# Moving the moment matmuls within a slot of the output phase

## The chip, the cores and the metric

The kernel runs on one core of a Trainium2 chip. The time is the device time of one execution in microseconds (us). TensorE is called PE in the rows, VectorE DVE, ScalarE ACT, GpSimd POOL, and SyncE SP. SP does no arithmetic here: it issues the DMAs.

## What is computed

The reference is a chain of blocks on a tensor of 16 images of 64 x 64 tokens with 128 channels. The change touches the last step of the attention block and the batch statistics that the block after it needs:

```python
attn1 = jax.nn.softmax(sim1, axis=-1)          # sim1 = q @ k_landmarks, 8 heads of 16, 64 landmarks
out = attn1 @ attn2_inv @ (attn3 @ v)          # attn2_inv @ (attn3 @ v) is ready before the output phase
res = conv_general_dilated(v, conv_w, ...)     # along the tokens, 33 taps per head
out = (out + res).reshape(...) @ w_out + b_out
t = t + out
...
Wx = jnp.einsum('bti,hi->bth', _ln_t(t), W)    # the ffn
mean = jnp.mean(flat, axis=0)                  # over all tokens of all images
var = jnp.var(flat, axis=0)
```

The mean and variance of `Wx` follow from the first and second moments of the normalised tokens. The kernel gathers these moments while it makes the tokens.

## The kernel before

The program runs its phases one after the other: group norm, the recurrent layer, landmarks, the pseudo-inverse, the output phase, and a last recurrence over the tokens. The edit lies in `output_phase` (from L1878).

The output phase goes over 16 images, each in 8 groups of 512 tokens. The work on one group is spread over several **slots**, and a slot (b, c) does one step each of several groups: 128 slots in all. On each engine a function `slot` writes out the order by hand, and semaphores tie the engines together. There is no scheduler. The names below are the tiles in the rows.

TensorE's slot, in its order before the change, with the line of each matmul:

- `scores` (L2171, L2175): the attention scores of group c, four banks of 512 columns (`o_bank_s`). They wait for ScalarE's negated maxima, and for its copies out of the banks that they overwrite: the third is the bank of the convolution (semaphore `convc`, set by ScalarE's copy at L2289).
- `row_maxima` r = 0 (L2152): half of the scores of group c + 1 in bf16, from which VectorE takes row maxima (L2355). Its banks are two, `o_bank_l`.
- `project` (L2211): the output projection of group c - 3 into `o_bank_x`.
- `row_maxima` r = 1 (L2152): the other half, into the same two banks. The second bank may be written only when VectorE has read two maxima of r = 0.
- `weigh` (L2185): the weighing of the values with the exponentials, which waits for ScalarE's four exponentials (L2318) and overwrites two of the score banks.
- `queries` (L2138) of group c + 3, `turn_maxima` (L2160) of group c + 1, `convolve` (L2197) for the next image, and `turn_convolved` (L2205), transposes of the convolved values of group c - 2.
- `moments` (L2224): 16 small matmuls of group c - 4 that add into `o_bank_m`, which is read once, at the phase's end. They wait for GpSimd's scaled tokens `o_u` (L2089), written in the slot's first microseconds.

ScalarE's slot: four exponentials (L2318), two scalings of the residual's base (L2302), the rounded queries (L2295), the two copies of the weighed values `o_even` and `o_odd` (L2310, L2312), the queries (L2280), the negated maxima (L2284), the convolved values (L2289), two more scalings.

VectorE's slot: the four maxima of group c + 1 (L2355), the residual of group c - 3 with its statistics (L2366 to L2372), the reciprocals of the packed denominators (L2386, which wait for a DMA), normalising (L2397), adding the convolved values (L2380, which waits for the transposes of `turn_convolved`), and merging (L2391). Of these, normalising and merging read two operands from SBUF.

GpSimd's slot: the mask (L2073), then variance plus epsilon (L2082), the power (L2084) and the scaled tokens (L2089) of group c - 3, then the base's bias (L2097).

SyncE's queue: the reciprocals are spread and broadcast through DRAM, and the next denominators are packed after that, so that one reciprocals instruction stands a whole chain of DMAs behind the one before it.

The last image has no `convolve`, and the first four slots have no `moments`.

Of the kernel before, what the change touches and what calls it, by code (L numbers as in the profile page):

```python
# [1877 lines left out]
def output_phase(nc, sems, R, E, K, xnt, tokens, vals, recips, scaled):  # L1878


    with ExitStack() as ctx:
# [47 lines left out]
        def nth(b, c):  # L1929

            return NG * b + c + 1

        def wait(eng, name, count):

            if count > 0:
                eng.wait_ge(s[name], count)
# [13 lines left out]
        def follows(c, k, last):  # L1950

            return c + k < NG or not last

        def precedes(c, k, first):

            return c >= k or not first
# [171 lines left out]
        def _(pe):  # L2128
# [5 lines left out]
            def queries(b, c):  # L2134

                pe.wait_ge(*loaded(s_xl, *at(b, c)))
                wait(pe, "qc", nth(b, c) - 1)
                nc.tensor.matmul(bank_q[:, :], w[:, :], xnT[c % 4][:, :], start=True, stop=True).then_inc(s["qm"], 1)  # L2138

            def row_maxima(b, c, r, q):  # L2140

                if r == 0:
                    wait(pe, "ql", nth(b, c))
                    wait(pe, "setup", SETUP * (b + (c == NG) + 1))
                    wait(pe, "neg", nth(b, c) - 1)
                for k in range(2):
                    for half in range(2):
                        if k == 0:
                            wait(pe, "max", GT * (nth(b, c) - 1) + 2 * r + half - 1)
                        rows, heads = slice(LM * half, LM * half + LM), slice(PAIRS_H * half, PAIRS_H * half + PAIRS_H)  # L2150
                        token = P * (2 * r + k)
                        ml = nc.tensor.matmul(bank_l[half][:, 2 * P * k:2 * P * k + 2 * P], q_lp[c % 2][rows, token:token + P],  # L2152
                                              kb_lp[q][rows, heads, :].rearrange("c h l -> c (h l)"), start=True, stop=True)
                        if k == 1:
                            ml.then_inc(s["lp"], 1)

            def turn_maxima(b, c):
                wait(pe, "max", GT * nth(b, c))
                for k in range(GT):
                    mt = nc.tensor.matmul(bank_l[0][:, P * k:P * k + P], m1[:, k, :], E.ident_lp[:, :], start=True, stop=True)  # L2160
                mt.then_inc(s["mt"], 1)

            def scores(b, c, q):

                wait(pe, "neg", nth(b, c))
                wait(pe, "denc", 2 * (nth(b, c) - 1))
                wait(pe, "qc", min(nth(b, c) + 2, B * NG))
                wait(pe, "convc", min(NG + nth(b, c) - 1, B * NG))
                for g in range(PAIRS_H):
                    rows = slice(QUAD * g, QUAD * g + QUAD)  # L2170
                    nc.tensor.matmul(bank_s[g][:, :], ind[rows, :, :].rearrange("c a l -> c (a l)"), negm[c % 2][rows, :],  # L2171
                                     start=True, stop=False)
                for g in range(PAIRS_H):
                    rows = slice(QUAD * g, QUAD * g + QUAD)
                    ms = nc.tensor.matmul(bank_s[g][:, :], kb[q][rows, :, :].rearrange("c a l -> c (a l)"), qT[c % 4][rows, :],  # L2175
                                          start=False, stop=True)
                ms.then_inc(s["s1"], 1)

            def weigh(b, c, q):

                wait(pe, "exp", PAIRS_H * nth(b, c))
                for h in range(2):
                    rows = slice(LM * h, LM * h + LM)
                    for g in range(PAIRS_H):
                        mp = nc.tensor.matmul(bank_pv[h][QUAD * g:QUAD * g + QUAD, :], zb[q][rows, g, :], p1[g][rows, :],  # L2185
                                              start=True, stop=True)
                mp.then_inc(s["pv"], 1)

            def convolve(b, c, out):

                half, pair = c // GT, c % GT
                pe.wait_ge(s_v[half], 128 * (b + 1))
                turns = out.rearrange("p (n e) -> p n e", e=2 * DH)
                for a in range(2):
                    h = 2 * pair + a
                    for side in range(2):
                        mm = nc.tensor.matmul(turns[LM * side:LM * side + LM, :, DH * a:DH * a + DH], bands[:, h, :],  # L2197
                                              v[half][side][:, :, (DH + 1) * h:(DH + 1) * h + DH], start=True, stop=True,
                                              skip_group_check=True)
                mm.then_inc(s["conv"], 1)  # L2200

            def turn_convolved(b, c, q):
                wait(pe, "res", nth(b, c) - 1)
                for k in range(GT):
                    mt = nc.tensor.transpose(bank_x[:, k, :], res[q][:, GT * (c % NG) + k, :], R.ident[:, :])  # L2205
                mt.then_inc(s["ct"], 1)

            def project(b, c):
                wait(pe, "add", nth(b, c))
                for k in range(GT):  # L2210
                    mt = nc.tensor.matmul(bank_x[:, k, :], oT[:, P * k:P * k + P], wo[:, :], start=True, stop=True)  # L2211
                mt.then_inc(s["wo"], 1)

            def moments(b, c):

                n = nth(b, c)
                wait(pe, "u", n)
                if n == 1:
                    pe.wait_ge(K.ready, K.PARTS + 2)
                    wait(pe, "centre", 2)  # L2220
                for k in range(GT):
                    for g in range(P // QUAD):
                        r = (g - k) % BLOCK_ROWS
                        mm = nc.tensor.matmul(bank_m[QUAD * g:QUAD * g + QUAD, FROM[r]:FROM[r] + WIDTH[r]],  # L2224
                                              u[c % 2][:, k, 1 + QUAD * r:1 + QUAD * r + QUAD], u[c % 2][:, k, 0:WIDTH[r]],
                                              start=n == 1 and k == 0, stop=n == B * NG and k == GT - 1, skip_group_check=True)
                mm.then_inc(s["moments"], 1)

            def slot(b, c, q, first, last):
                scores(b, c, q)  # L2230
                nq = q if c + 1 < NG else 1 - q
                if follows(c, 1, last):
                    row_maxima(b, c + 1, 0, nq)
                if precedes(c, 3, first):
                    project(b, c - 3)
                if follows(c, 1, last):
                    row_maxima(b, c + 1, 1, nq)
                weigh(b, c, q)
                if follows(c, 3, last):
                    queries(b, c + 3)  # L2240
                if follows(c, 1, last):
                    turn_maxima(b, c + 1)
                if not last:
                    convolve(b + 1, c, bank_conv[:, :])
                if precedes(c, 2, first):
                    turn_convolved(b, c - 2, q if c >= 2 else 1 - q)
                if precedes(c, 4, first):
                    moments(b, c - 4)

            nc.tensor.matmul(bank_m[:, 0:C], E.avg[:, :], fw[:, :], start=True, stop=True).then_inc(s["centre"], 1)  # L2250
            pe.wait_ge(s_band, 16)
# [8 lines left out]
            turn_maxima(0, 0)  # L2260
            wait(pe, "convc", NG)
            each_image(pe, slot)
            project(B - 1, NG - 3)
            turn_convolved(B - 1, NG - 2, 1)
# [594 lines left out]
```

## Time and profile before

| | us |
|---|---|
| median of 3 runs | 5903.51 |
| lowest, highest | 5903.4, 5907.3 |
| the profiled execution | 5913.64 |
| its span (first to last instruction) | 5911.8 |
| output phase, first to last slot's work, by the stage rows | about 1078 |

The stages of the trace are told apart by the lines that run. The output phase takes the stretch from 2515 to 3593 us of the span; what stands before and after it uses none of the changed lines. A slot is read from one engine at a time: the timeline of TensorE gives each slot from one `scores` (L2171) to the next, and the timelines of the other engines over the same stretch show what each was doing meanwhile.

### The profile page before, as it was taken

Reading aid. Unit: us, or ns where it says so; the run is one execution under the profiler, and the core shown is the slowest. Engines: PE = TensorE matmul, PEld = TensorE weight load, DVE = VectorE, ACT = ScalarE, POOL = GpSimd, SP = SyncE. Lnnn points to the kernel's source line nnn. Section 1 sums busy time; section 2 is a strip of 40 time slices with the busy share of each in tenths; the row PEclk is TensorE's granted clock in tenths of the full one; section 3 lists DMA queues with packets and bytes.
Section 4 is the critical chain, followed back from the end, with each engine's and each line's share of the span. In section 5 each row is a group of like instructions: output and inputs, shape, how many; then the busy total and the mean of one; then the engine's idle time right before and its main releaser. Section 6 shows DMA issues by size and latency. Waiting matters only on the chain. (4 is left out here: it accounts for less than half of the span.)

```text
span 5911.8 us, 223297 instructions
## 1 busy us (share of the span) xinstructions
PE 5253.6 (89%) x97395; PEld 3278.2 (55%) x97488; DVE 3071.2 (52%) x8152; ACT 3138.0 (53%) x9108; POOL 1523.0 (26%) x1905
## 2 busy tenths in 40 slices
PE   5599999997899998799999997888888888888888
PEld 4599888896566666744444444333333333333333
DVE  8677777775788886568888883111111111111111
ACT  6465555565677776378888883333333333333333
POOL 2100000002888874256666662000000000000000
PEclk7899999999999999999999998999999999999999
DMA  9631111225777773467777762111111111111100
GB/s 389 270 115 58 58 58 60 84 77 183 245 245 243 231 243 105 102 175 203 202 203 202 204 173 66 33 34 32 32 34 33 32 32 35 32 32 32 35 18 24
DMA packets 773031, 689.32 MB, mean 117 GB/s; under 512 B 67056, under 2 KB 663024, under 8 KB 767984
## 3 DMA queue, kind: packets, MB, share of 16 engines
q1 hardware_dynamic: 754672, 575.39, 32.6%
q0 software_dynamic: 14672, 95.16, 4.0%
q8 instruction: 743, 12.17, 0.9%
q10 hardware_dynamic: 2736, 4.89, 0.2%
q14 instruction: 208, 1.70, 0.1%
HBM read 392.17 MB, written 274.89 MB: 113 GB/s over the span
## 5 line engine op out<-in xcount | busy, mean ns | idle before, releaser
L2797 ACT ACTIVATE f_y<-f_acc 128x16 f32<-128x16 f32 x4096 | 754.7, 184 | 1542.5 <-PE f_acc L2739 1542.5
L2739 PEld LDWEIGHTS f_acc<-f_y,f_vT 128*32 128x32 f32 x32768 | 645.2, 108 | 1438.7 <-ACT f_y L2797 1437.0
L2739 PE MATMUL f_acc<-f_y,f_vT 128*32 128x16 f32 x32768 | 1046.1, 193 | 279.6 <-issue 1.5
L2697 PE MATMUL f_junk<-f_idle 128*32 128x512 bf16 x8400 | 832.5, 376 | 0.0
L2579 DVE COPY f_zT<-f_zt 128x512 f32<-128x512 f32 x124 | 85.8, 692 | 1138.4 <-PE f_zt L2653 1138.4
L2355 DVE TENSOR_REDUCE o_m<-o_bank_l 128x8 bf16<-128x512 f32 x512 | 329.7, 686 | 132.4 <-PE o_bank_l L2152 130.0
L2572 DVE TENSOR_SCALAR f_wxn<-f_wxp,f_scale,f_shift 128x512 f32<-128x512 f32 x126 | 102.1, 811 | 509.0 <-PE f_wxp L2667 508.9
L1299 ACT ACTIVATE a_p<-a_s 128x512 f32<-128x512 f32 x502 | 259.3, 602 | 153.0 <-PE a_s L1166 151.2
L2318 ACT ACTIVATE o_p<-o_bank_s 128x512 f32<-128x512 f32 x512 | 264.4, 602 | 142.0 <-PE o_bank_s L2175 142.0
L533 POOL DMA_DIRECT2D hidden<-l_h x46 | 34.7, 756 | 1162.1 <-DVE l_hsum L790 961.6
L712 ACT ACTIVATE l_gate<-l_pf,r_ctx 128x256 f32<-128x256 f32 (+7 forms) x512 | 202.5, 446 | 229.1 <-PE l_pf L643 228.8
L2592 DVE SCALAR_TENSOR_TENSOR f_sum<-f_u,f_std,f_turned 128x128 f32<-128x128 f32 x512 | 143.6, 344 | 317.9 <-PE f_turned L2690 317.9
L2697 PEld LDWEIGHTS f_junk<-f_idle 128*32 128x32 bf16 x8400 | 250.0, 99 | 0.0
L1359 DVE TENSOR_REDUCE a_m3p<-a_s 128x1 f32<-128x512 f32 x360 | 223.6, 684 | 50.8 <-PE a_s L1126 49.4
L633 PE MATMUL l_pio<-l_x,r_k_lm 128*128 128x256 f32 (+7 forms) x1024 | 239.0, 356 | 0.2 <-ACT l_gate L729 0.2
L633 PE MATMUL l_pf<-l_x,r_k_lm 128*128 128x256 f32 (+7 forms) x1024 | 238.9, 356 | 0.0
L647 PE MATMUL l_pio<-l_hsum,r_ctx 128*128 128x256 f32 (+7 forms) x1024 | 238.8, 356 | 0.0
L2302 ACT ACTIVATE o_base<-o_base,r_loss,r_gain 128x128 f32<-128x128 f32 x512 | 225.8, 498 | 0.3 <-DMA o_base<-tokens 0.3
L2690 PE MATMUL f_turned<-f_ident,f_y 128*32 128x128 f32 x4096 | 221.1, 290 | 0.5 <-DVE f_sum L2592 0.5
L1017 POOL TENSOR_TENSOR a_r<-a_vare,a_half 128x8 f32<-128x8 f32 x128 | 209.6, 1638 | 10.0
L712 ACT ACTIVATE l_gate<-l_pio,r_ctx 128x256 f32<-128x256 f32 (+7 forms) x512 | 203.4, 450 | 13.9
L2679 PE MATMUL f_acc<-f_wxn,f_ident 128*32 128x128 f32 x4096 | 207.1, 274 | 0.7 <-issue 0.7
(323 smaller groups left out, 11517.6 us busy)
## 6 DMA issues: line engine op xcount, KB each, us to landing
o_v<-vals SPq DMA_DIRECT2D x256, 272.0 KB, 3.4
a_hid<-hidden SPq DMA_DIRECT2D x112, 520.0 KB, 5.0
hidden<-l_h POOLq DMA_DIRECT2D x46, 1040.0 KB, 6.6
l_x<-skew SPq DMA_DIRECT2D x46, 1024.0 KB, 5.2
vals<-a_v SPq DMA_DIRECT2D x128, 272.0 KB, 3.4
gn_x<-in_x SPq DMA_DIRECT2D x16, 2048.0 KB, 17.4
a_xin<-in_x SPq DMA_DIRECT2D x128, 256.0 KB, 5.1
tokens<-a_t SPq DMA_DIRECT2D x128, 256.0 KB, 3.4
```

What stands on the lines that cost most here:

```text
L633: mm = nc.tensor.matmul(banks[c][g][:, :, rows], w[W[g]], xs, start=g in (0, 2, 3), stop=False, skip_group_check=True)
L647: mm = nc.tensor.matmul(banks[c][g][:, :, rows], w[U[g]], hsum[:, lanes[c], rows], start=False, stop=True, skip_group_check=True)
L712: nc.scalar.activation(gate[:, g, lanes[c], rows], banks[c][g][:, :, rows], ACT.Tanh if g == 2 else ACT.Sigmoid, bias=bias[BI[g]]).then_in ...
L1299: nc.scalar.activation(p3[c % 2][g][:, :], score_bank(i, c, g), ACT.Exp).then_inc(s["exp"], 1)
L1359: nc.vector.tensor_reduce(m3p[:, g, c:c + 1], bank[:, :], AX.X, ALU.max).then_inc(s["mx"], 1)
L2302: nc.scalar.activation(bs[c % 4][:, k, :], bs[c % 4][:, k, :], ACT.Identity, scale=R.gain[:, b, n:n + 1], bias=R.loss[:, b, n:n + 1]).then ...
L2318: nc.scalar.activation(p1[g][:, :], bank_s[g][:, :], ACT.Exp).then_inc(s["exp"], 1)
L2355: nc.vector.tensor_reduce(m1[:, 2 * r:2 * r + 2, LM * half:LM * half + LM].rearrange("p k (g r) -> p k g r", r=QUAD)[:, :, :, 0:2], bank_l ...
L2690: mt = nc.tensor.matmul(turned[g % 2][rows, b % 4, :], y[q][:, rows, b], ident[:, :], start=True, stop=True)
L2697: nc.tensor.matmul(junk[rows, :], idle[:, 0:QUAD], idle[:, :], start=True, stop=True)
L2739: mm = nc.tensor.matmul(acc[k % 2][rows, t, :], vT[:, rows], before, start=False, stop=True, skip_group_check=True)
L2797: nc.scalar.activation(y[q][:, step, :], acc[step // RC % 2][:, step % RC, :], ACT.Sigmoid).then_inc(s_y, 1)
```

## The change

In TensorE's slot, the call of `moments(b, c - 4)` moves from the last place to the place between `row_maxima` r = 1 and `weigh`. No instruction is added or removed, and the order on ScalarE, VectorE, GpSimd and SyncE is the same.

```diff
@@ -2235,6 +2235,8 @@
                     project(b, c - 3)
                 if follows(c, 1, last):
                     row_maxima(b, c + 1, 1, nq)
+                if precedes(c, 4, first):
+                    moments(b, c - 4)
                 weigh(b, c, q)
                 if follows(c, 3, last):
                     queries(b, c + 3)
@@ -2244,8 +2246,6 @@
                     convolve(b + 1, c, bank_conv[:, :])
                 if precedes(c, 2, first):
                     turn_convolved(b, c - 2, q if c >= 2 else 1 - q)
-                if precedes(c, 4, first):
-                    moments(b, c - 4)
```

TensorE before, the first slot that has moments, from its scores to the first moment matmuls:

```order
L2171 MATMUL o_bank_s<-o_negm,o_ind 128x512 x4
L2175 MATMUL o_bank_s<-o_qT,o_kb 128x512 x4
L2152 MATMUL o_bank_l<-o_kb_lp,o_q_lp 128x256 x4
L2211 MATMUL o_bank_x<-o_wo,o_oT 128x128 x4
L2152 MATMUL o_bank_l<-o_kb_lp,o_q_lp 128x256 x4
L2185 MATMUL o_bank_s<-o_p,o_zb 32x512 x8
L2138 MATMUL o_bank_s<-o_xnT,o_wq 128x512
L2160 MATMUL o_bank_l<-o_ident_lp,o_m 128x128 x4
L2197 MATMUL o_bank_s<-o_v,o_bands 64x16x16 x4
L2205 MATMUL o_bank_x<-r_ident,o_res 128x128 x4
L2224 MATMUL o_bank_m<-o_u 32x33
L2224 MATMUL o_bank_m<-o_u 32x65
```

TensorE now, the same slot, from its scores to the first moment matmuls:

```order
L2171 MATMUL o_bank_s<-o_negm,o_ind 128x512 x4
L2175 MATMUL o_bank_s<-o_qT,o_kb 128x512 x4
L2152 MATMUL o_bank_l<-o_kb_lp,o_q_lp 128x256 x4
L2211 MATMUL o_bank_x<-o_wo,o_oT 128x128 x4
L2152 MATMUL o_bank_l<-o_kb_lp,o_q_lp 128x256 x4
L2224 MATMUL o_bank_m<-o_u 32x33
L2224 MATMUL o_bank_m<-o_u 32x65
```

The moments stand where the weighing stood, and the weighing comes behind them. TensorE now, from the last moment matmul to the next slot's scores:

```order
L2224 MATMUL o_bank_m<-o_u 32x33
L2185 MATMUL o_bank_s<-o_p,o_zb 32x512 x8
L2138 MATMUL o_bank_s<-o_xnT,o_wq 128x512
L2160 MATMUL o_bank_l<-o_ident_lp,o_m 128x128 x4
L2197 MATMUL o_bank_s<-o_v,o_bands 64x16x16 x4
L2205 MATMUL o_bank_x<-r_ident,o_res 128x128 x4
L2171 MATMUL o_bank_s<-o_negm,o_ind 128x512 x4
```

The next scores (L2171) now follow the transposes (L2205) directly.

## Rows read from the trace of the kernel before

**Rows 1.** Stages of the output phase: stretch, us, busy us by engine, PEclk, DMA, GB/s.

```profile
2561.30:3510.30 949.00, 917.92 (x10908) 469.42 (x10911) 782.82 (x1973) 784.15 (x1626) 636.00 (x640) 1.00 0.72 200
3510.30:3593.50 83.20, 65.48 (x835) 38.22 (x830) 61.86 (x167) 47.05 (x100) 54.12 (x54) 0.86 0.38 107
```

**Rows 2.** Timeline, PE, one steady slot: start us, us, what, [idle before].

```profile
2856.58 0.40 PE L2171 MATMUL o_bank_s<-o_negm,o_ind 32*128 32x512 bf16 x4
...
2859.18 0.75 PE L2152 MATMUL o_bank_l<-o_kb_lp,o_q_lp 64*128 64x256 bf16 x4
2860.03 1.09 PE L2185 MATMUL o_bank_s<-o_p,o_zb 64*32 64x512 f32 x16
...
2863.37 0.66 PE L2205 MATMUL o_bank_x<-r_ident,o_res 128*128 128x128 f32 x4
2863.95 0.77 PE L2224 MATMUL o_bank_m<-o_u 128*32 128x33 f32 x32
2864.66 0.40 PE L2171 MATMUL o_bank_s<-o_negm,o_ind 32*128 32x512 bf16 x4
```

**Rows 3.** Timeline, ACT, the same slot: the exponentials.

```profile
2857.91 2.06 ACT L2318 ACTIVATE o_p<-o_bank_s 128x512 f32<-128x512 f32 x4 [1.14 <-PE o_bank_s L2175]
```

**Rows 4.** Timeline, PE, the last slot that has no moments.

```profile
2553.66 0.40 PE L2171 MATMUL o_bank_s<-o_negm,o_ind 32*128 32x512 bf16 x4 [0.20 <-ACT o_res L2289]
...
2557.09 1.09 PE L2185 MATMUL o_bank_s<-o_p,o_zb 64*32 64x512 f32 x16
...
2561.32 0.40 PE L2171 MATMUL o_bank_s<-o_negm,o_ind 32*128 32x512 bf16 x4 [0.20 <-ACT o_res L2289]
```

**Rows 5.** Timeline, ACT, that slot's copy of the convolved values.

```profile
2560.57 0.60 ACT L2289 ACTIVATE o_res<-o_bank_s 128x512 f32<-128x512 f32 x1 [0.21 <-PE o_bank_s L2197]
```

**Rows 6.** Timeline, DVE, the end of that slot: adding and merging.

```profile
2561.21 0.69 DVE L2380 TENSOR_TENSOR o_oT<-o_att,o_bank_x 128x512 f32<-128x512 f32 x1 [0.23 <-DVE o_att L2397]
2561.81 0.74 DVE L2391 SCALAR_TENSOR_TENSOR o_att<-o_odd,o_keep,o_pvs 128x512 f32<-128x512 f32 x1
```

**Rows 7.** Timeline, DVE, the steady slot of rows 2.

```profile
2856.65 0.74 DVE L2391 SCALAR_TENSOR_TENSOR o_att<-o_odd,o_keep,o_pvs 128x512 f32<-128x512 f32 x1
2858.19 1.29 DVE L2355 TENSOR_REDUCE o_m<-o_bank_l 128x8 bf16<-128x512 f32 x2 [0.80 <-PE o_bank_l L2152]
...
2861.07 0.68 DVE L2366 TENSOR_TENSOR o_t<-o_bank_x,o_base 128x512 f32<-128x512 f32 x1
```

**Rows 8.** Timeline, POOL, the scaled tokens at this slot's start and the next one's.

```profile
2857.02 1.27 POOL L2089 TENSOR_TENSOR o_u<-o_t,k_rstd 128x512 f32<-128x512 f32 x1
...
2865.12 1.25 POOL L2089 TENSOR_TENSOR o_u<-o_t,k_rstd 128x512 f32<-128x512 f32 x1
```

**Rows 9.** Timeline, DVE, a slot in which the merging took long.

```profile
3052.53 1.61 DVE L2391 SCALAR_TENSOR_TENSOR o_att<-o_odd,o_keep,o_pvs 128x512 f32<-128x512 f32 x1
3054.07 1.28 DVE L2355 TENSOR_REDUCE o_m<-o_bank_l 128x8 bf16<-128x512 f32 x2
```

**Rows 10.** Timeline, POOL, the scaled tokens of that slot.

```profile
3052.56 1.04 POOL L2089 TENSOR_TENSOR o_u<-o_t,k_rstd 128x512 f32<-128x512 f32 x1
```

**Rows 11.** Timeline, PE, that slot: scores, then the rest of the second row maxima.

```profile
3052.12 0.40 PE L2171 MATMUL o_bank_s<-o_negm,o_ind 32*128 32x512 bf16 x4
...
3055.40 0.39 PE L2152 MATMUL o_bank_l<-o_kb_lp,o_q_lp 64*128 64x256 bf16 x3 [0.32 <-DVE o_m L2355]
```

**Rows 12.** Timeline, DVE, a slot with late reciprocals.

```profile
2590.05 0.68 DVE L2366 TENSOR_TENSOR o_t<-o_bank_x,o_base 128x512 f32<-128x512 f32 x1
...
2592.49 0.35 DVE L2386 RECIPROCAL o_rec_packed<-o_den_packed 128x32 f32<-128x32 f32 x1 [0.40 <-DMA o_den_packed<-o_odd]
...
2594.02 1.12 DVE L2391 SCALAR_TENSOR_TENSOR o_att<-o_odd,o_keep,o_pvs 128x512 f32<-128x512 f32 x1
```

**Rows 13.** Timeline, POOL, the scaled tokens of that slot.

```profile
2593.55 1.04 POOL L2089 TENSOR_TENSOR o_u<-o_t,k_rstd 128x512 f32<-128x512 f32 x1
```

**Rows 14.** Waits from 2561 to 3510 us: total, times, longest.

```profile
DVE o_rec_packed L2386 <- DMA o_den_packed<-o_odd: 29.1, 41, 2.2
```

**Rows 15.** Timeline, PE: scores at both ends of one of the long slots.

```profile
2626.02 0.40 PE L2171 MATMUL o_bank_s<-o_negm,o_ind 32*128 32x512 bf16 x4
...
2635.40 0.39 PE L2171 MATMUL o_bank_s<-o_negm,o_ind 32*128 32x512 bf16 x4
```

**Rows 16.** Timeline, PE, the scores of the last image's first slot.

```profile
3510.28 0.40 PE L2171 MATMUL o_bank_s<-o_negm,o_ind 32*128 32x512 bf16 x4
```

## The prediction, made before the changed kernel ran

> **What bounds the kernel now.** I read the stages first, then one slot engine by engine. The changed lines run in the output phase alone. There TensorE is busy for 917.9 of 949.0 us with the clock granted in full, and VectorE and ScalarE for 783 and 784 [rows 1], so TensorE's order sets the pace and the other two have about a sixth of the time to spare. Next comes TensorE's timeline of a steady slot. From one scores (L2171) to the next it takes 2864.66 - 2856.58 = 8.08 us [rows 2]; in the neighbouring slots 8.08 and 8.10 take turns, and I calculate with 8.09. I cut the slot at the weighing (L2185). The first part, scores to weighing, takes 3.45 us [rows 2]. It ends with the exponentials, which begin 1.33 after the scores and are done at 3.39 [rows 3]. The second part, weighing to the next scores, takes 4.63 us, and its last piece is the moments, 2864.66 - 2863.95 = 0.71 us [rows 2]. TensorE waits nowhere in the second part.
>
> The first four slots have no moments, and their rows show what binds once they are gone from the slot's end. The second part took 2561.32 - 2557.09 = 4.23 us there [rows 4], and ended with a wait of 0.20 for ScalarE's copy of the convolved values, which ran until 2561.17 [rows 5]. The scores overwrite that copy's bank. This copy stands behind four other ScalarE instructions that begin when the weighing ends, so it moves with the weighing. The slots beside it show 4.19; I use 4.21.
>
> **The change part by part.** Nothing is added or removed. The moments' 0.71 us leave the second part and enter the first one.
>
> *Second part.* 0.71 us go, but only 4.64 - 4.21 = 0.43 is won, since the wait for the convolved copy appears in their place. The copy had been hidden by the moments alone.
>
> *First part.* The second row maxima end at 2859.93, 3.35 after the scores, and the exponentials end at 3.39 [rows 2, 3]. The idle time into which the moments could go is thus 0.1 us (2859.93 to 2860.03). There is also a pause of 0.36 inside the second row maxima (four of these matmuls take 0.75 here and 0.39 unhindered, as the three and the lone one of rows 11 show), where TensorE waits for VectorE's second maximum. The moments stand behind that pause, not in it. So the weighing starts 3.35 - 0.07 + 0.71 = 3.99 after the scores, where 0.07 is the overlap by which each group follows the last (the transposes end at 2864.03, and the moments start at 2863.95). The exponentials then end 0.6 us before they are wanted, which gives nothing back. The first part grows by 0.54.
>
> A slot would then take 3.99 + 4.21 = 8.20 us, 0.11 more than now, if VectorE kept up as before. It doesn't, by these rows.
>
> *VectorE against GpSimd.* The merging (L2391) starts 0.60 after the adding (L2380), and the adding follows the transposes, which come a fixed time after the weighing. In the slot without moments it started 4.72 us after the weighing (2561.81 against 2557.09) and so 0.49 after the next scores [rows 4, 6]. With moments it starts just 0.07 after the scores (2856.65 against 2856.58), since the scores themselves are later [rows 2, 7]. The scaled tokens (L2089) on GpSimd hang from something else: they start 4.05 us after the residual (2865.12 against 2861.07), and that starts 1.14 after the second row maxima end [rows 2, 7, 8]. Now the merging has a lead of 0.37 (2856.65 against 2857.02), takes 0.74, and GpSimd's instruction is the one that is stretched, to 1.27 from 1.04 [rows 7, 8, 10].
>
> After the change the merging starts at 0.49 of a slot, and the scaled tokens at 1.14 + 4.05 - 0.64 - 4.21 = 0.34, where 0.64 is what lies between the end of the row maxima and the weighing. GpSimd is first, by 0.15. What this costs stands in two places. With a lead of 0.03 only, the merging took 1.61 and ended 0.54 after GpSimd's instruction (3054.14 against 3053.60) [rows 9, 10]. With GpSimd 0.47 ahead it took 1.12 and ended 0.55 behind it (2595.14 against 2594.59) [rows 12, 13]. So the merging ends at 0.34 + 1.04 + 0.55 = 1.93 of the slot. The first maximum follows 0.07 before that end, as at 3054.07 [rows 9]: at 1.86, where now it starts at 1.61 (2858.19) [rows 7]. The second row maxima then end 1.72 later (3055.79 against 3054.07) [rows 9, 11], at 3.58 in place of 3.35. The slot takes 3.58 - 0.07 + 0.71 + 4.21 = 8.43 to 8.44 us. The delay moves residual, scaled tokens, weighing and merging alike, so the 0.15 stays and the collision returns in the next slot.
>
> For VectorE's wait the Trainium skill has a rule (page "SBUF — State Buffer", section "Who interferes with whom"): a VectorE instruction with two SBUF inputs and a GpSimd instruction that reads SBUF exclude each other, and the second to issue waits until the first is finished. This agrees with which instructions were stretched. It would have the merging start anew at GpSimd's end, with its whole 0.74 behind it, 0.19 later than the 0.55 of rows 9 and 10; by it a slot would take 8.63 and the sum would come to some +48 us. The rows decide here.
>
> *Not all slots collide.* Where the reciprocals wait for their DMA (41 waits of 29.1 us in all [rows 14]), normalising comes later and the power on GpSimd gets through before it: the scaled tokens then start 3.50 after the residual (2593.55 against 2590.05 [rows 12, 13]) instead of 4.05. In the changed kernel they would end at -0.21 + 1.04 = 0.83 of the slot, and the merging at 0.83 + 0.55 = 1.38, early enough for the maxima at 1.61. Such a slot takes 8.20. Of the 116 slots with moments outside the last image, 42 were of this kind. The chain of DMAs from one reciprocals instruction to the next is as long as before while the slots are longer, so there are fewer of them. I carried the distances between reciprocals of the trace through the changed slot times; some 85 slots came out at 8.44, some 30 at 8.20 to 8.4 (8.25 in the mean), and one long one.
>
> *Long slots.* Some slots take much more than 8.09 where the broadcast reciprocals come late (9.38 from 2626.02 to 2635.40 [rows 15]). All excess over 8.09 together is 10.5 us. The adding waits for the transposes, and now these come 0.54 later as seen from the residual, so lateness up to that is absorbed. I keep one of 9.4.
>
> *Moved past nothing else.* The moments wait for scaled tokens that are done about 1.4 us into the slot and are wanted at 3.3, so this wait costs nothing, with 1.9 us of cover; what queues behind it is the weighing. Their bank is read at the phase's end. SP's queue is not touched.
>
> *Last image.* It has no convolution, so the negated maxima bind in the second part instead. Its seven slots grow by up to 0.5 each, but in the trace they are stretched by late reciprocals anyway (83 us for the tail with the last slots [rows 1]). I take +1, between 0 and +3.
>
> *Sum.* Before: 3510.28 - 2561.32 = 948.96 us for 116 slots [rows 4, 16], 8.18 each. After: 85 x 8.44 + 30 x 8.25 + 9.4 = 974.3. Difference +25.3, with the last image +26. On the profiled execution, span 5911.8 and time 5913.64, that gives 5937.8 and 5939.6; on the median of 5903.51 it gives 5929.5, say **5930 us** (+0.45%). That execution lies 10 us above the median, and I have no row that puts this difference in the output phase.
>
> **The rivals.**
>
> *No collision: no change.* The 0.15 us between GpSimd and the merging is a difference of two sums of eight terms. If the moments take 0.19 less in their new place, or the convolved copy 0.19 less, the merging gets ahead and a slot takes 8.20. For it: in the trace of before the merging is ahead in two slots of three. Against: a lead of 0.03 wasn't enough [rows 9, 10], and no single term is uncertain by 0.1. Price: 116 x 8.20 = 951.2, with two long slots 954, +1: +3 to +6 us, 5908.
>
> *Faster.* The moments could fill the time in which TensorE waits before the weighing, 0.1 for the exponentials and 0.36 for the maximum, which is what a total of waits suggests. They would then cost the first part nothing, and the second wins its 0.43: 116 x 7.66 = 889, 5903.5 - 60 = 5844. The pause would have to lie behind the moments. It lies ahead of them and the idle time there is 0.1 [rows 2, 3]. This decides from a first part under 3.88.
>
> *Slower than forecast.* Every slot collides: 116 x 8.44 = 979.0, +31, 5935. If the merging is held back for its whole length, as in the rule above, 5952.
>
> **How the numbers follow.** A measurement of this kernel can tell about 0.2%, 11.8 us, from no change. Chances: collision in most slots 0.75, no collision 0.18, faster 0.04, the whole-length case 0.03. The collision case alone spans 5917 to 5942 (half of the slots at 8.20, or all at 8.44 with 0.05 more each). The range takes in the no-collision case down to 5906 and goes to 5945. Faster than -0.2%: 0.04. Within: 0.18. Slower: 0.78.
>
> **What the changed profile would show.** In a steady slot: weighing 3.99 to 4.2 after the scores; scores that follow the transposes with an idle time of about 0.2 released by the convolved copy; no wait of the weighing for the exponentials; the merging at about 1.4 us instead of 0.75, starting 0.15 behind the scaled tokens; the wait for VectorE's maximum in the second row maxima longer by a quarter microsecond; slots of 8.44 in most places and 8.20 where the reciprocals waited; fewer waits of the reciprocals than 41. The forecast is wrong if the merging stays at 0.75 with GpSimd's instruction stretched (no change), or if the weighing keeps 3.45.

## The result and the profile after

| | before | after |
|---|---|---|
| median, us | 5907.30 (5 runs) | 5939.63 (5 runs) |
| lowest, highest | 5903.40, 5914.07 | 5935.92, 5943.66 |
| ratio, 95% interval | | 1.0054 [1.0039, 1.0068] |
| span of the profiled execution | 5911.8 | 5939.1 |
| the 116 slots of [rows 4, 16] | 948.96 | 973.63 |

The kernel became slower by 32 us. 5930 was forecast, with a range of 5906 to 5945. In the profiled executions the spans differ by 27.3 us, and 24.7 of these lie in the 116 slots with moments outside the last image. The rest isn't the edit's: in the profiles of this study the first slot began anywhere between 2527 and 2538 us, whatever the output phase held. I therefore compare variants by those 116 slots, and give the median beside them. Each of these sums is from one profiled execution, so I read nothing into a difference of a few microseconds between two of them; each ratio of an experiment is to the kernel before on the same chip.

The stage row of after answers to [rows 1]: stretch, us, busy us of PE, PEld, DVE, ACT and POOL, PEclk, DMA, GB/s.

```profile
2566.40:3540.00 973.60, 917.61 (x10904) 474.27 (x10905) 826.46 (x1973) 785.37 (x1625) 667.04 (x640) 1.00 0.70 196
```

TensorE and ScalarE are as busy as before (917.9, 784.2), at the full clock. VectorE counts 44 us more and GpSimd 31 more, with the same number of instructions. So some of theirs take longer: the merging adds up to 158.6 us where it was 98.9, and GpSimd's bias of the base (L2097), which stands right behind the scaled tokens, to 196.9 where it was 166.5. The scaled tokens themselves take less, 122.6 us where it was 138.7. The timeline of TensorE shows a slot, as [rows 2] did (start us, us, what, [idle before]).

```profile
2868.39 0.40 PE L2171 MATMUL o_bank_s<-o_negm,o_ind 32*128 32x512 bf16 x4 [0.20 <-ACT o_res L2289]
...
2870.99 0.28 PE L2152 MATMUL o_bank_l<-o_kb_lp,o_q_lp 64*128 64x256 bf16 x1
2871.57 0.39 PE L2152 MATMUL o_bank_l<-o_kb_lp,o_q_lp 64*128 64x256 bf16 x3 [0.30 <-DVE o_m L2355]
2871.89 0.77 PE L2224 MATMUL o_bank_m<-o_u 128*32 128x33 f32 x32
2872.59 1.09 PE L2185 MATMUL o_bank_s<-o_p,o_zb 64*32 64x512 f32 x16
...
2875.93 0.66 PE L2205 MATMUL o_bank_x<-r_ident,o_res 128*128 128x128 f32 x4
2876.78 0.40 PE L2171 MATMUL o_bank_s<-o_negm,o_ind 32*128 32x512 bf16 x4 [0.20 <-ACT o_res L2289]
```

The moments take 2872.59 - 2871.89 = 0.70 us in the new place, as in the old one. The weighing comes 4.20 after the scores, where it came at 3.45. It was 2876.78 - 2872.59 = 4.19 from there to the next scores, where it was 4.63, and the scores now wait 0.20 for ScalarE's copy of the convolved values. The second row maxima stand still for VectorE in the middle and end at 2871.96, 3.57 after the scores and not 3.35.

VectorE's timeline over the same slot says why (it answers to [rows 6, 7]):

```profile
2868.28 0.69 DVE L2380 TENSOR_TENSOR o_oT<-o_att,o_bank_x 128x512 f32<-128x512 f32 x1 [0.79 <-DVE o_att L2397]
2868.89 1.43 DVE L2391 SCALAR_TENSOR_TENSOR o_att<-o_odd,o_keep,o_pvs 128x512 f32<-128x512 f32 x1
2870.24 1.28 DVE L2355 TENSOR_REDUCE o_m<-o_bank_l 128x8 bf16<-128x512 f32 x2
```

And GpSimd's (it answers to [rows 8]):

```profile
2868.73 1.04 POOL L2089 TENSOR_TENSOR o_u<-o_t,k_rstd 128x512 f32<-128x512 f32 x1
2869.72 1.71 POOL L2097 TENSOR_TENSOR o_base<-o_base,o_bout 128x512 f32<-128x512 f32 x1
```

The scaled tokens start at 2868.73, 0.34 after the scores. The merging starts at 2868.89, 0.16 behind them, and takes 1.43 us. It ends 0.55 after the scaled tokens (2870.32 against 2869.77). The maxima start 1.85 into the slot instead of 1.61. In the next slot the merging stands 0.13 behind and the slot takes 8.45; the two kinds take turns. In the trace of before the merging led by 0.37 and took 0.74 [rows 7, 8].

The table of waits of after, over the 116 slots, holds the rest (total, times, longest):

```profile
PEld o_bank_l L2152 <- DVE o_m L2355: 54.3, 116, 0.5
PE o_bank_s L2171 <- ACT o_res L2289: 23.4, 116, 0.2
DVE o_rec_packed L2386 <- DMA o_den_packed<-o_odd: 2.8, 9, 0.6
```

The row maxima wait 0.47 us a slot for VectorE's maxima, and the scores wait for the convolved copy in all 116 slots. The reciprocals waited 9 times for 2.8 us, where it had been 41 times for 29.1 [rows 14].

### The profile page after: what moved, and what is told of

Same layout as the page of the kernel before. It is cut to its first block and busy times, and to the rows that moved or that the text cites. A ratio compares the mean times of both kernels' runs of the same rounds, so it can differ in the third digit from the quotient of the medians.

```text
span 5939.1 us, 223297 instructions
## 1 busy us (share of the span) xinstructions
PE 5252.7 (88%) x97395; PEld 3284.8 (55%) x97488; DVE 3115.5 (52%) x8152; ACT 3138.1 (53%) x9108; POOL 1552.9 (26%) x1905
## 5 line engine op out<-in xcount | busy, mean ns | idle before, releaser
L2097 POOL TENSOR_TENSOR o_base<-o_base,o_bout 128x512 f32<-128x512 f32 x128 | 213.9, 1671 | 4.0 <-ACT o_base L2302 4.0
```

## The experiments

The theory, *collision*: the move alone costs 0.11 us a slot (0.54 lost in the first part, 0.43 won in the second), and most slots lose another 0.24, since the merging on VectorE and the scaled tokens on GpSimd hold each other up and the order of their starts has turned round. The first rival, *order alone*: VectorE is late behind TensorE for a reason of its own, and GpSimd has no part in it. The second doubts a step: the moments could have been hidden in the first part after all.

### GpSimd is given more to do: nap

The changed kernel, with a memset of a tile that nobody reads:

```diff
+                pool.memset(nap[:, :], 0.0)                  # nap: [P, 256]
                 pool.tensor_tensor(u[c % 2][:, :, 1:1 + C], t2s[c % 2][:, :, :], ...
```

> The changed kernel, with one memset of an unused tile of 128 x 256 fp32 put on GpSimd right before its scaled tokens: work is added, nothing else moves. Theory (collision): in the changed kernel the scaled tokens start at 0.37 of a slot and the merging at 0.50, so the merging waits and a slot takes 8.40 to 8.45. If the memset delays the scaled tokens by more than 0.15 us, the merging comes first and takes 0.75, the second row maxima end at 3.35, and a slot takes 8.17 to 8.20. Over 116 slots that is 27 us less than the changed kernel: added work makes it faster, at about 5912, +5 us against the kernel before. If the memset takes less than 0.13, nothing changes. Rival (TensorE's order alone, the merging is late for a reason of its own): the slots stay at 8.43, 5938 or more. Rival (GpSimd is itself late for something): slower than the changed kernel.

Measured: 5918.3 us, ratio to before 1.0015 [1.0006, 1.0025]; 952.7 us for the 116 slots, 20.9 less than the changed kernel. GpSimd's timeline:

```profile
2863.98 0.31 POOL L2090 MEMSET o_nap<- 128x256 f32 x1
2864.25 1.55 POOL L2091 TENSOR_TENSOR o_u<-o_t,k_rstd 128x512 f32<-128x512 f32 x1
```

VectorE's:

```profile
2864.16 0.75 DVE L2393 SCALAR_TENSOR_TENSOR o_att<-o_odd,o_keep,o_pvs 128x512 f32<-128x512 f32 x1
2865.27 1.29 DVE L2357 TENSOR_REDUCE o_m<-o_bank_l 128x8 bf16<-128x512 f32 x2 [0.37 <-PE o_bank_l L2154]
```

The merging now leads by 0.09 and takes 0.75. GpSimd's instruction is the one that is stretched, to 1.55, which hurts nobody. 107 of the slots take 8.17 to 8.20, the other nine more. The 27 us that were expected were not quite reached. More work on GpSimd made the kernel faster, and order alone cannot explain that.

### The same with a short memset: short_nap

```diff
-        nap = m.sb("o_nap", [P, 256])
+        nap = m.sb("o_nap", [P, 64])
```

> As the run nap, with a memset of 64 columns in place of 256. The long one delayed the scaled tokens by 0.25 us. Theory (collision, decided by who starts first): this one delays them by 0.05 to 0.10, and in the changed kernel they lead the merging by 0.12 to 0.15; so they still come first, the merging still waits and ends 0.55 after them, that is later by the delay. A slot gets longer by it, 8.47 to 8.53 in place of 8.40 to 8.45, 979 to 988 over the 116 slots, 5945 to 5953. Rival (any work on GpSimd spreads the two apart gradually): between the changed kernel and nap, 8.3 to 8.4. The same edit with more columns took 21 us away, so a sign that turns round with the size of the memset would speak for the order of starts alone.

Measured (4 runs): 5946.4 us, ratio 1.0063 [1.0047, 1.0079]; 982.05 us for the 116 slots, 8.4 more than the changed kernel. GpSimd's timeline, and the merging of the same slot:

```profile
2910.67 0.15 POOL L2090 MEMSET o_nap<- 128x64 f32 x1
2910.78 1.04 POOL L2091 TENSOR_TENSOR o_u<-o_t,k_rstd 128x512 f32<-128x512 f32 x1
```

```profile
2910.82 1.54 DVE L2393 SCALAR_TENSOR_TENSOR o_att<-o_odd,o_keep,o_pvs 128x512 f32<-128x512 f32 x1
2912.28 1.27 DVE L2357 TENSOR_REDUCE o_m<-o_bank_l 128x8 bf16<-128x512 f32 x2
```

The delay is 0.08, and the scaled tokens still lead, by 0.04. The merging takes 1.54 and ends 0.54 after them. In 101 slots the mean is 8.51 us, against 8.43 in the 98 colliding slots of the changed kernel. A delay of 0.08 costs 8 us and one of 0.25 gives 21 back: the sign turns where the order of the starts turns.

### The merging is moved out of the way: merge_first, before_merge_first

```diff
                 if precedes(c, 2, first):
                     normalise(b, c - 2)
-                    add_convolved(b, c - 2)
                 if precedes(c, 1, first):
                     merge(b, c - 1)
+                if precedes(c, 2, first):
+                    add_convolved(b, c - 2)
```

On the changed kernel:

> The changed kernel, with VectorE's merging of group c - 1 put between normalising and adding, so that it no longer starts behind the transposes, some 0.5 after the scores, but right after normalising, 2.85 after the residual. Theory (collision): the merging then meets the power on GpSimd (2.95 after the residual) with a lead of 0.1, and the scaled tokens later start while VectorE has no instruction with two operands from SBUF; the maxima start at 1.61, a slot takes 8.17 to 8.20, 27 us less than the changed kernel, about 5912. Rival (TensorE's order alone): 8.43 stays.

Measured: 5913.53 us, ratio 1.0012 [1.0003, 1.0021]; 950.0 us for the 116 slots, 23.6 less than the changed kernel. VectorE's timeline:

```profile
2866.74 0.74 DVE L2391 SCALAR_TENSOR_TENSOR o_att<-o_odd,o_keep,o_pvs 128x512 f32<-128x512 f32 x1
2867.55 0.69 DVE L2380 TENSOR_TENSOR o_oT<-o_att,o_bank_x 128x512 f32<-128x512 f32 x1
2869.27 1.29 DVE L2355 TENSOR_REDUCE o_m<-o_bank_l 128x8 bf16<-128x512 f32 x2 [1.03 <-PE o_bank_l L2152]
```

The maxima start 1.61 after the scores at 2867.66, released by TensorE alone. It is 3.98 from scores to weighing and 4.20 from there on in the median: the 8.17 to 8.20 that a slot takes with the move and without the collision. That is 0.10 more than in the kernel before, and yet all 116 slots together take only 1.0 us more (950.0 against 948.96): the kernel before had 10.5 us of slots that were longer than 8.09, and these have all but gone. The same edit on the kernel before:

> The kernel before with the merging put ahead of the adding, the edit that took 24 us from the changed kernel. Theory (that edit removes the collision and nothing else): in the kernel before the merging mostly came first anyway, so at most the long slots change; 8.08 to 8.10 a slot, 938 to 949 over 116 slots, 0 to -10 us. Rival (merging early is a gain of its own): -20 us or more, 5885.

Measured: 5911.91 us, ratio 1.0002 [0.9992, 1.0011]; 946.95 us for the slots, 2.0 less. The merging placed early is no gain of its own. It only takes away a collision, and there was little of one.

### The moments ahead of the pause: in_pause

The moments one place further up than in the changed kernel:

```diff
                     project(b, c - 3)
+                if precedes(c, 4, first):
+                    moments(b, c - 4)
                 if follows(c, 1, last):
                     row_maxima(b, c + 1, 1, nq)
```

> The moments stand one place earlier than in the changed kernel: between the projection and the second row maxima, ahead of the pause in which TensorE waits for VectorE's second maximum. My step said that the moments gain nothing in the first part because the pause lies ahead of them. Theory: here they fill the pause. Projection ends at 2.67, moments until 3.31, the four row-maxima matmuls then take 0.32 unhindered, weighing at 3.63 in place of 3.98 to 4.23. The second part stays at 4.2 (the convolved copy). 7.84 by TensorE's order; the merging leads the scaled tokens by 0.5, no collision. Then the chain of DMAs between reciprocals (7.4 to 9.5, where it is seen, 8.2 in the middle) becomes the next bound: I expect 7.9 to 8.1 a slot, 5885 to 5905, faster than the kernel before by 0 to 20 us. Rival (the first part cannot take the moments anywhere): slots of 8.2 or more, 5915 and above.

Measured: 5899.09 us, ratio 0.9989 [0.998, 0.9998]; 936.9 us for the 116 slots, 12.1 less than before. TensorE's timeline:

```profile
2581.78 0.40 PE L2171 MATMUL o_bank_s<-o_negm,o_ind 32*128 32x512 bf16 x4 [0.20 <-ACT o_res L2289]
...
2584.38 0.77 PE L2224 MATMUL o_bank_m<-o_u 128*32 128x33 f32 x32
2585.08 0.39 PE L2152 MATMUL o_bank_l<-o_kb_lp,o_q_lp 64*128 64x256 bf16 x4
2585.41 1.09 PE L2185 MATMUL o_bank_s<-o_p,o_zb 64*32 64x512 f32 x16
...
2589.63 0.40 PE L2171 MATMUL o_bank_s<-o_negm,o_ind 32*128 32x512 bf16 x4 [0.20 <-ACT o_res L2289]
```

The four row-maxima matmuls run through in 0.39 where they took 0.75, the weighing comes 3.63 after the scores, and the slot takes 7.85. So the same 0.70 us of matmuls cost 0.54 in the first part behind the pause and 0.18 ahead of it. The forecast's step was right: behind the row maxima the moments gain nothing. Ahead of them there is no collision in such a slot either: the merging starts 0.59 before the scaled tokens (2582.36 against 2582.95). Of the possible 40 us, though, only 12 came. The waits hold the rest, and there are two kinds:

```profile
DVE o_rec_packed L2386 <- DMA o_den_packed<-o_odd: 43.4, 65, 2.2
PE o_bank_s L2197 <- DMA o_v<-vals: 9.3, 10, 1.6
```

99 slots take 7.89 in the mean, 4 some 8.5, and 13 take 122.3 us together, 9.4 each. In six of the 13 the first part is long (5.1 to 5.5 us) and no load is waited for: TensorE's projection waits for VectorE's adding, as in the slot of [rows 15]. In the other seven TensorE itself waits in the second part, in `convolve`, for the load of the next image's values, as here in a slot of 9.30:

```profile
2852.26 1.11 PE L2197 MATMUL o_bank_s<-o_v,o_bands 128*64 128x256 f32 x8 [0.98 <-DMA o_v<-vals]
```

The ten slots with that wait hold 12 of the 27.5 us by which the 116 slots exceed 7.84 each. In the kernel before there were three such slots, with 1.9 us of waits. Both kinds are waits for DMAs that the longer slots seldom met. That the chain from one reciprocals instruction to the next takes longer than such a slot fits the first kind (7.3 to 9.4 us where the reciprocals waited); what makes the loads late, no run shows.

### Half and half, and nearly none: halves, few_moments

```diff
                     project(b, c - 3)
+                if precedes(c, 4, first):
+                    moments(b, c - 4, range(2))
...
                 if precedes(c, 4, first):
-                    moments(b, c - 4)
+                    moments(b, c - 4, range(2, GT))
```

> Two of the four token tiles' moments (8 of 16 matmuls, 0.35 us) stand between the projection and the second row maxima, the other two stay at the slot's end. Theory: the first half fills the pause of 0.36 for the second maximum, so the weighing stays at 3.45. The second half covers the wait for the convolved copy: weighing to scores 3.93 + 0.35 = 4.28 in place of 4.64. A slot takes 7.73 by TensorE's order, if nothing else binds; I expect the DMA chain between the reciprocals to bind then, at 7.9 to 8.1, 5885 to 5905. The second part at 4.28 would show that the copy needs 0.3 of cover and that 0.35 of it is as good as 0.71. Rival (moments cost their 0.71 wherever they stand): 8.09, 5905.

Measured: 5901.65 us, ratio 0.9991 [0.9982, 1.0], which reaches no change; 942.0 us for the 116 slots. Most slots take 7.9, and ten take over 9, with both kinds of waits again. The weighing stayed at 3.45 as expected. The second part was 4.46, not 4.28, since half of the moments takes more than half of the time:

```profile
2697.78 0.59 PE L2224 MATMUL o_bank_m<-o_u 128*32 128x33 f32 x16
2698.31 0.39 PE L2152 MATMUL o_bank_l<-o_kb_lp,o_q_lp 64*128 64x256 bf16 x4
2698.63 1.09 PE L2185 MATMUL o_bank_s<-o_p,o_zb 64*32 64x512 f32 x16
...
2702.58 0.58 PE L2224 MATMUL o_bank_m<-o_u 128*32 128x97 f32 x16
2703.10 0.39 PE L2171 MATMUL o_bank_s<-o_negm,o_ind 32*128 32x512 bf16 x4
```

0.53 and 0.52 us, against 0.70 for all of them. The code suggests why: the four column groups of the array work side by side, each gets widths of 33, 65, 97 and 129 columns over the four token tiles, and over two tiles one group has 97 and 129 in a row while another has 33 and 65. The run three_one_two below gives two more points.

The kernel before with the moments all but left out, to price them at the slot's end:

```diff
+                        if 0 < n - 1 < B * NG - 1 and (k, g) != (GT - 1, P // QUAD - 1):
+                            continue
                         mm = nc.tensor.matmul(bank_m[...], ...)
```

> The kernel before, with 15 of the 16 moment matmuls of each group left out (all but those of the first and the last group): this leaves work out, and the moments in the result are not those of all tokens. It shows what the moments cost at the slot's end. Theory: the scores then wait for ScalarE's copy of the convolved values, as in the first four slots: 7.64 a slot with weighing to scores 4.2, so that the moments' 0.71 us cost 0.45 there, and 0.26 of it was cover. A slot shorter than the chain of DMAs between reciprocals cannot be kept up, so the mean will be 7.8 to 8.0. Rival (the moments cost their full 0.71): weighing to scores 3.93.

Measured, one run: 5894.24 us (the kernel before on that chip: 5909.48); 930.8 us for the 116 slots, 8.02 each. TensorE's timeline, and ScalarE's copy of the convolved values in the same slot:

```profile
2586.88 0.40 PE L2171 MATMUL o_bank_s<-o_negm,o_ind 32*128 32x512 bf16 x4
2590.31 1.09 PE L2185 MATMUL o_bank_s<-o_p,o_zb 64*32 64x512 f32 x16
2593.68 0.66 PE L2205 MATMUL o_bank_x<-r_ident,o_res 128*128 128x128 f32 x4
2594.26 0.25 PE L2226 MATMUL o_bank_m<-o_u 128*32 128x33 f32 x2
2594.53 0.40 PE L2171 MATMUL o_bank_s<-o_negm,o_ind 32*128 32x512 bf16 x4
```

```profile
2593.79 0.60 ACT L2291 ACTIVATE o_res<-o_bank_s 128x512 f32<-128x512 f32 x1 [0.21 <-PE o_bank_s L2197]
```

Weighing to scores is 4.22 us and not 3.93, and the slot 7.65. TensorE's rows alone don't tell why, since the matmul that is left runs until 2594.51 and would give the same 4.2. The copy decides: it ends at 2594.39, and the scores start 0.14 behind it, as they do where the wait is printed (0.15 in [rows 4, 5]). So even with 15 of 16 matmuls gone the second part keeps 4.2, and the moments cost some 0.44 of their 0.70 in the old place. Again the reciprocals waited (82 times, 59.0 us), and the mean was 8.02: 41 slots took 7.65, and four took 10.9 to 13.2, which this one run does not explain. Slots under 8.0 are possible, but none of these kernels kept them up in the mean.

### The chain of DMAs: two_buffers, pause_buffers, pause_two, three_one_two

Spreading the reciprocals waits for the last broadcast, because both use one DRAM buffer. With two buffers, in the kernel before:

```diff
-    recips = scratch("recips", (HEADS, 512))
+    recips = scratch("recips", (2, HEADS, 512))
...
-                    sp.wait_ge(s_rden, 16 * (nth(b, c) - 1))
+                    sp.wait_ge(s_rden[c % 2], 16 * (4 * b + c // 2))
```

> The kernel before, with two buffers in DRAM for the spread reciprocals, so that a spread waits for the broadcast before the last and not for the last one (70 us of SyncE's waits stand there). The order on TensorE is that of before. Theory: the late reciprocals and the slots over 8.09 come from this chain; nearly all slots take 8.08 to 8.10, 938.5 over the 116 slots in place of 949.0, -8 to -11 us, about 5896. Rival (the lateness is that of the transfers themselves, not of the chain): no change, 5905.

Measured: 5910.31 us, ratio 0.9998 [0.9989, 1.0007]; 946.7 us for the 116 slots, 2.3 less. The 8 to 11 us that were expected did not come. The reciprocals still waited 39 times (24.7 us). SyncE's wait for the broadcast (70.1 us in the trace of before) is gone, and its wait for the reciprocals grew from 88.3 to 150.7. The former was thus not what made them late. Together with the moments in the pause:

> All moments in the pause as in in_pause, and two DRAM buffers for the reciprocals, with SyncE's issue order as before: the packing is not moved ahead of the broadcast. Theory: moving the packing ahead made the broadcasts late in pause_two (84 waits of the normalising, 80 us), and without that the two buffers help a little: 930 to 937 over 116 slots, -12 to -19 us against the kernel before in the same stretch, about 5890. Rival (the two buffers were what slowed pause_two): 5900 and above with waits of the normalising for its broadcast.

Measured: 5901.9 us, ratio 0.9986 [0.9977, 0.9995]; 941.8 us for the 116 slots, no better than in_pause with 936.9. The expected 930 to 937 was missed, and TensorE again waited for the values (8.5 us, 11 times).

Two further kernels had the packing of the denominators ahead of the broadcast as well:

```diff
                 if precedes(c, 1, first):
                     spread(b, c - 1)
+                pack(b, c)
...
                 if precedes(c, 1, first):
                     broadcast(b, c - 1)
-                pack(b, c)
```

> All moments in the pause (between the projection and the second row maxima, as in the run in_pause), with the two DRAM buffers, and with the packing of the denominators issued before the broadcast instead of behind it. Theory: in_pause had 7.82 to 7.84 by TensorE's order (weighing at 3.62, second part 4.20) and lost 29 us over 116 slots to late reciprocals; without them 116 x 7.83 = 908, -41 us against the kernel before, about 5865. Rival (another bound lies just below 8.0, for example VectorE's own work or the loads of the values): -15 to -25, 5880 to 5890.

> As pause_two, but three of the four token tiles' moments stand in the pause and one stays at the slot's end. Theory: the second part needs 0.26 of cover, which one tile's four matmuls give (the widest has 129 columns, about 0.3 us), so it stays at 4.2; the first part loses what the fourth tile took, about 0.1, since the four column groups share the load unevenly: 7.7 to 7.8 a slot, -41 to -52 us against the kernel before, 5853 to 5865. Rival (split moments cost as much more as they save, as in the run halves, where a half took 0.52 of 0.71): 7.83 or more, no better than pause_two.

Measured: 5944.41 us, ratio 1.0053 [1.004, 1.0067], and 5944.18, ratio 1.0052 [1.0038, 1.0066]; 977.0 and 978.7 us for the 116 slots. Both expectations fell, by 80 us. In pause_two the waits show what had taken the reciprocals' place:

```profile
DVE o_att L2400 <- DMA o_rden<-recips: 80.2, 84, 2.2
```

The same row of pause_buffers, which differs only in SyncE's order:

```profile
DVE o_att L2400 <- DMA o_rden<-recips: 2.1, 2, 1.2
```

The order alone costs 35 us over the 116 slots. By the code the packing, two DMAs which wait for ScalarE's copies of the weighed values, now stands ahead of the broadcast in SyncE's queue, and normalising waits for the broadcast. TensorE's waits for the values grew as well, to 16.9 us in 17 slots. What would shorten the chain remains open.

The slots that these waits left alone (under 8.0 us) still answer what three_one_two asked. They take 7.85 there (50 of pause_two: 7.84), with 3.56 in the first part and 4.28 in the second. Its rival was right: what the split saves in the first part it loses in the second. Its moments:

```profile
2700.87 0.71 PE L2226 MATMUL o_bank_m<-o_u 128*32 128x33 f32 x24
2701.52 0.39 PE L2154 MATMUL o_bank_l<-o_kb_lp,o_q_lp 64*128 64x256 bf16 x4
...
2705.76 0.42 PE L2226 MATMUL o_bank_m<-o_u 128*32 128x65 f32 x8
2706.11 0.39 PE L2173 MATMUL o_bank_s<-o_negm,o_ind 32*128 32x512 bf16 x4
```

Three tiles take 0.65 us and one takes 0.35. With halves that makes four points: one, two, three and four tiles take 0.35, 0.53, 0.65 and 0.70, and the column group with the most to do has 129, 226, 291 and 324 columns. Each step is about 0.18 us for 100 columns of that group, the last one a little less. The times thus follow the fullest group and not the number of matmuls.

## Why the prediction was right, point by point

*Second part.* 4.21 was calculated, and in the median it was 4.20, with the wait of 0.20 for the convolved copy. The copy had been covered by the moments alone; few_moments shows the same 4.2, set by the copy, with one of them left.

*First part.* 3.99 without collision and 4.22 with it: measured 3.98 and 4.21. The moments kept their 0.70 us and nothing absorbed them.

*Collision.* GpSimd first by 0.15, merging ending at 1.93 of the slot, maxima at 1.86, a slot of 8.43 to 8.44: measured 0.16, 1.93, 1.85 and 8.40 in the slot shown, and 0.13, 1.95, 1.88 and 8.45 in the next. nap, short_nap and merge_first show that this is the cause of the greater part: 21 to 24 of the 24.7 us. The move without the collision comes to about +1, as the rival "no collision" had it (+3 to +6 with the last image).

*How many.* 85 slots at 8.44 and 30 at 8.25 were put into the sum, with one of 9.4, 974.3 us in all. It was 98 (8.36 and over) with a mean of 8.43, 18 with a mean of 8.21, none long, 973.6 us in all. That the sum met the measurement within 1 us is luck: the errors cancelled. The reciprocals waited less than I had assumed (9 times), which fits slots that are longer than most passes through the chain of DMAs. This made more slots collide, and it removed the long one. The long slots of before had also been put down to late reciprocals alone; in three of them (8.5 to 8.9 us) TensorE waited for the load of the values.

*Last image.* +1 was put in, -1.0 was measured (51.55 to 50.52 for its first seven slots). The first three grew from 6.9 to between 7.3 and 7.5, as forecast, but one of 10.0 us, in which the reciprocals had waited 1.3, was gone. Between the profiles of all variants the seven slots took 50.5 to 51.6, so the sign shows nothing.

*The rest.* The medians differ by 32 us, 6 more than the sum, and the interval of the ratio, 23 to 40 us, takes in both. 5 us of the 27.3 between the profiled spans stand ahead of the output phase (first scores at 2535.8 and 2530.7), where no instruction was changed. Between profiles of other variants that time varied as much, so the output phase didn't cause it. Two figures around the sum don't follow from its terms: half of the slots at 8.20 would give 5920 as the lower end, not 5917, and slots of 8.63 in 85 of 116 would give +42 us, not +48. Neither decided anything.

*The page's rule.* The Trainium skill ("SBUF — State Buffer", section "Who interferes with whom") has the one that starts first keep the other blocked. This agrees with which instruction was stretched, but for three pairs, in which the merging led by 0.02 to 0.035 us and was stretched all the same. That the merging would then have its whole 0.74 behind GpSimd's end was the forecast's own reading, and it would have given slots of 8.63. In the colliding slots shown it ended 0.54 to 0.55 after GpSimd's instruction, and the slots took 8.40 to 8.53.

## What to carry to other kernels

Work that fills a wait must stand ahead of that wait in the engine's own order. The same moments cost 0.54 us behind the row maxima and 0.18 ahead of them, and a table of waits doesn't tell these apart; the timeline does. Before moving work off the end of a slot, look at what it covers there (here a copy of 0.6 us on another engine, whose wait took back 0.28 of the 0.71 us). And check how far an instruction of VectorE with two operands from SBUF starts from one of GpSimd that reads SBUF: here a shift of 0.25 us between them decided over 21 to 24 us.

## What the runs showed of the hardware that was not expected

- The collision is decided by hundredths of a microsecond. The merging kept its 0.75 us with a lead of 0.09 over GpSimd's instruction (nap), and took 1.61 with a lead of 0.03 [rows 9, 10] and 1.54 when it was 0.04 behind (short_nap). Over all traces it kept 0.74 to 0.75 in each of the pairs where it led by 0.04 to 0.2, and was stretched in each where it led by less or came up to 0.15 behind. However long it was stretched there, it ended 0.54 to 0.55 after GpSimd's instruction.
- A memset on GpSimd had no part in the collision that could be seen. In nap the two overlapped by 0.13 us and the merging kept its 0.75. The memset delayed the next instruction by 0.25 us with 256 columns and by 0.08 with 64.
- Four of the sixteen moment matmuls took 0.35 us, eight 0.53, twelve 0.65 and all sixteen 0.70, in step with the columns of the fullest column group.
- A slot shortened by 0.25 us on TensorE (in_pause) returned 0.10 on average, because 13 of 116 slots grew to 9.4 us behind DMAs (the reciprocals' and the values') that no slot of the changed kernel waited for so long. Of the versions tried that compute everything, in_pause (5899.09 us against 5905.82 for the kernel before on the same chip, ratio 0.9989 [0.998, 0.9998]) and pause_buffers (ratio 0.9986 [0.9977, 0.9995]) are the fastest, and can't be told apart. Both gains are below what I had called tellable from no change.
